# Softmax row sums inverted through 32x32 transposes on VectorE

## The chip, the cores and the metric

The kernel runs on one core of a Trainium2 chip. Its engines work side by side and each takes its own instructions in order: TensorE (PE in the profile; PEld is its weight load), VectorE (DVE), ScalarE (ACT), GpSimd (POOL), and SyncE (SP), which issues the DMAs. They meet through semaphores. The time is the device time of one execution in microseconds (us), and what is compared is the median of several executions.

## The reference

The input x is 8 images of 512 channels by 32x32 pixels, in fp32. With t the 1024 tokens of an image:

```
xn   = group_norm(x)                              # 32 groups
mask = sigmoid(relu(mean(xn) @ w1 + b1) @ w2 + b2) > 0.5      # per image and channel
hyp  = logmap0(mhsa(expmap0(xn * mask), hdn weights))
euc  = mhsa(xn * (1 - mask), eu weights)
out  = x + hyp + euc

mhsa(x): q, k, v = split(t @ w_qkv + b_qkv)       # 8 heads of 64
         attn    = softmax(q @ k.T / 8)           # 1024 x 1024 per head
         out     = (attn @ v) @ w_o + b_o
```

So there are 16 attentions (8 images, 2 branches), each with 8 heads. The change is about the softmax's denominator: one number per head and query, whose reciprocal multiplies the 64 outputs of that head and query.

## The kernel before, in words

The outer loops run over the image i (0 to 7) and the branch t (0 and 1). In a branch, heads go in 4 pairs and queries in 2 halves of 512, which makes 8 phases ph = 2 * pair + half; a phase has 8 key tiles of 128, and one unit g is one key tile for both heads of the pair. BATCHES is 32: a batch b is two units, so a phase lasts 4 batches. All engines follow the same hand-written timetable in b; nothing is planned at run time.

For each unit TensorE makes the scores (`scores`, L1449), ScalarE their exponentials (`exps`, L871, tile `probs`, 4 slots), TensorE multiplies them by v into `acc_ps` (`prob_v`, L1463), and GpSimd adds them up over the key tiles into `sums` (`probs_sum`, L690). In the same batches TensorE makes what the next pair needs: the q and k projections (`qk_tile`, L1364) and, in two slots per batch (`max_slot`, L1413), products whose row maxima VectorE takes (`mxp`, L1201). Both slots of a batch use the same two PSUM banks (0 and 1), so the second slot's matmuls wait for the first slot's reduction, and the first slot of the next batch waits for the second's. `combine` (L1211) and `turn` (L1224, eight 32x128 transposes) shape the maxima.

At the end of a phase, `denominator` (L1477) multiplies `sums` by a 128x64 matrix of ones into an auxiliary bank. Its output is 128 partitions by 512 queries, and the 64 partitions of one head all hold the same number. ScalarE copies it to `den` (`den_copy`, L882), VectorE inverts it in place (`recip`, L1285), GpSimd multiplies the drained attention output `o_raw` by it (`mult`, L697), ScalarE and VectorE split the product into a rounded part and a rest (`o_hi` L887, `o_lo` L1290), and the output projection (`o_tile`, L1364 with w_o) reads both. Output tiles 0 to 3 need the first query half, tiles 4 to 7 the second.

`recip` is called twice per phase, each time for 256 of the 512 columns, in batches 4 * ph + 6 and 4 * ph + 8 (the second call of phase 6 in batch 31), and behind the second max slot of the batch. Phase 7 is inverted behind the last batch, with all 512 columns in one call. VectorE's order in a batch:

```
max_slot, combine                        # first slot
o_lo, small steps, lows(b - 1)           # qk_lo of the projections
max_slot, combine                        # second slot
recip(ph, parts)                         # even batches, and 31
scale_x and other steps, turn
```

`Count.at(i, n)` turns "n-th event of image i" into a semaphore value; `c_rec` counts quarters of a phase's inversion (RECIP_PARTS = 4), and `mult` waits for all four. SyncE begins the program by incrementing each semaphore of the list COUNTS once (L520), before its first DMA (L566).

Of the kernel before, what the change touches and what calls it, by code (L numbers as in the profile page):

```python
# [13 lines left out]
P = 128  # L14
HALF = 512
# [3 lines left out]
PAIRS = HEADS // 2  # L19
# [43 lines left out]
BLOCK = 32  # L63
# [23 lines left out]
RECIP, RECIP_PARTS = [6, 8], 4  # L87
# [8 lines left out]
def followed(i):  # L96

    return i != B - 1
# [7 lines left out]
def wanted(i, t, p):  # L106

    return p < PAIRS or t != 1 or followed(i)
# [3 lines left out]
def max_slot_at(b, j):  # L112

    return divmod(2 * b + j - MAX_FROM, 16)
# [11 lines left out]
def phase_at(b, what):  # L126

    ph, r = divmod(b - what, 4)
    return ph if r == 0 and 0 <= ph < 2 * PAIRS - 1 else None
# [12 lines left out]
def projections(b):  # L142

    out = [("v", m) for m in range(2 * b, 2 * b + 4) if b % 2 == 0 and m < NT]
    for p in range(2, PAIRS + 2):
        out += [("qk", p, k) for k in range(4) if b == min(8 * p + QK_AT[k], BATCHES)]
    return out
# [81 lines left out]
def build(nc, x, w1, b1, w2, b2, hw_qkv, hb_qkv, hw_o, hb_o, ew_qkv, eb_qkv, ew_o, eb_o, out):  # L229
    ctx = ExitStack()  # L230
    with ctx:
        ctx.enter_context(nc.allow_non_contiguous_dma(reason="biases, once"))

        def sb(name, shape, dt=F32):
            return ctx.enter_context(nc.sbuf_tensor(name, shape, dt))
# [30 lines left out]
        den = sb("den", [P, 2, HALF])  # L266

        mxw = sb("mxw", [P, 2, NT // 2, BLOCK], F32R)
        mxp = sb("mxp", [P, 2, NT, 2])
        group_mean = sb("group_mean", [P, P])  # L270
        ones = sb("ones", [P, HD])
        stats = sb("stats", [P, KC, 2, 6])
# [23 lines left out]
        def frees(tiles, e, n=None):  # L296

            return sum(by == e for _, by, _ in tiles[:n])
# [8 lines left out]
        def sem(name):  # L307
            return ctx.enter_context(nc.semaphore(name))

        def counted(name, per, before=0):  # L310
            return Count(sem(name), per, before)
# [16 lines left out]
                 for q in range(XIN)]  # L328
# [16 lines left out]
        c_free = {e: counted(n, frees(AUX, e), frees(FIRST, e))  # L345
                  for e, n in (("A", "aux_read_by_scalar"), ("D", "aux_read_by_vector"),
                               ("Q", "qk_lo_made"))}
        c_hi = counted("qk_hi_made", 32, 8)
        c_mx = counted("max_made", 16, 2)

        c_turn = [counted(f"max_rows_made{h}", 8, 1 - h) for h in range(2)]
        c_neg = [counted(f"max_rows_rounded{h}", 8, 1 - h) for h in range(2)]
        c_score = counted("scores_made", NSC)
        c_exp = counted("probs_made", NSC)
        c_pv = counted("probs_multiplied", 2 * TILES)
        c_sum = [counted(f"probs_summed{h}", NSUM) for h in range(2)]
        c_raw = counted("o_drained", 16)
        c_rec = counted("recip_made", 16 * RECIP_PARTS)
        c_on = counted("o_normal", 16)
        c_ohi = counted("o_hi_made", 16)  # L360
        c_olo = counted("o_lo_made", 16)
        c_sq = counted("y_squared", 8)
# [3 lines left out]
        c_dstep = counted("vector_step", DVE_STEPS, DVE_FIRST)  # L366
        c_astep = counted("scalar_step", ACT_STEPS, ACT_FIRST)
        COUNTS = [*c_wqk, c_wv, c_wo, *c_xin, c_xfree, c_ss, c_yread, c_ysc, c_ysm, c_xlo, c_xm, c_xg, c_keep, c_xa, c_pe_in, c_d2a, c_a2d, c_yd2a, c_ya2d, c_aux,
                  *c_free.values(), c_hi, c_mx, *c_turn, *c_neg, c_score, c_exp, c_pv, *c_sum, c_raw, c_rec, c_on, c_ohi, c_olo, c_sq,
                  c_sqf, *c_x, *c_vst, c_dstep, c_astep]  # L370

        def bank(name):
# [7 lines left out]
        def aux_made(eng, i, name):  # L380

            eng.wait_ge(c_aux.sem, c_aux.at(i, at(i, name)[1] + 1))
            return bank(name)

        def aux_read(eng, i, name):

            tiles, n = at(i, name)
            e = tiles[n][1]
            eng.wait_ge(c_free[e].sem, c_free[e].at(i, frees(tiles, e, n + 1)))
# [37 lines left out]
        def token_half(h):  # L427
            return slice(h * HALF, (h + 1) * HALF)
# [24 lines left out]
        def y_square(k):  # L453

            return probs[:, SLOTS_P - 2 + k % 2, 0:HALF]
# [509 lines left out]
        def _(dve):  # L965
# [31 lines left out]
            def rows(ap):  # L997
                return ap.rearrange("p (r w) -> p r w", w=W)
# [278 lines left out]
            for i in range(B):  # L1277
                steps[0] = 0
                for t in range(2):

                    def recip(ph, parts):
                        n = 8 * t + ph
                        aux_read(dve, i, (t, "den", ph))
                        first, last = (parts[k] * HALF // RECIP_PARTS for k in (0, 1))
                        dve.reciprocal(den[:, ph % 2, first:last], den[:, ph % 2, first:last]).then_inc(c_rec.sem, parts[1] - parts[0])  # L1285

                    def o_lo(ph):
                        p, h = ph // 2, ph % 2
                        dve.wait_ge(c_ohi.sem, c_ohi.at(i, 8 * t + ph + 1))
                        dve.scalar_tensor_tensor(o_t[:, 1, p, token_half(h)], o_raw[:, ph % 2, :],  # L1290
                                                 bias_q[:, t, 2, p:p + 1], o_t[:, 0, p, token_half(h)].bitcast(F32),
                                                 ALU.add, ALU.subtract).then_inc(c_olo.sem, 1)

                    def lows(b):
                        for f in projections(b):
                            if f[0] == "qk" and wanted(i, t, f[1]):
                                qk_lo(i, t, f[1], f[2])

                    def y_done(k, t):
                        if t:  # L1300
                            ps = aux_made(dve, i, (1, "o", k))
                            dve.wait_ge(c_yread.sem, c_yread.at(i, k + 1))
                            dve.scalar_tensor_tensor(v_y[:, k, :], ps, bias_o[:, 1, k % KC:k % KC + 1], v_y[:, k, :],
                                                     ALU.add, ALU.add).then_inc(c_free["D"].sem, 1)
                        else:
                            dve.wait_ge(c_sq.sem, c_sq.at(i, k + 1))
                            dve.tensor_reduce(ss_y[:, k * ROWS:(k + 1) * ROWS], rows(y_square(k)), AX.X,
                                              ALU.add).then_inc(c_sqf.sem, 1)

                    for b in range(BATCHES):  # L1310
                        if t == 0 and b - 1 in GATE_BATCH and followed(i):
                            gate_read(i, t, GATE_BATCH[b - 1])
                        for j in range(2):
                            p, s = max_slot_at(b, j)
                            if wanted(i, t, p):
                                max_slot(i, t, p, s)
                                if s in HALF_DONE:
                                    combine(i, t, p, HALF_DONE.index(s))
                            if j == 0:
                                if t and b == Y_LAST:  # L1320
                                    y_done(7, 0)
                                if phase_at(b, LOW) is not None:
                                    o_lo(phase_at(b, LOW))
                                if t:
                                    y_scale_step(i, b)
                                    operand_step(i, t, b)
                                else:
                                    gate_step(i, b)
                                if b:
                                    lows(b - 1)  # L1330
                        for ph, parts in recips(b):
                            recip(ph, parts)
                        if t:
                            operand_tail(i, t, b)
                        else:
                            gate_tail(i, t, b)
                        if turn_at(b, TURN_AT) and wanted(i, t, turn_at(b, TURN_AT)[0]):
                            turn(i, t, *turn_at(b, TURN_AT))
                    o_lo(2 * PAIRS - 3)
                    lows(BATCHES - 1)  # L1340
                    o_lo(2 * PAIRS - 2)
                    lows(BATCHES)
                    if not closing(i, t):
                        y_done(0, t)
                    recip(2 * PAIRS - 1, (0, RECIP_PARTS))
                    if closing(i, t):
                        y_done(0, t)
                    y_done(1, t)
                    o_lo(2 * PAIRS - 1)
                    for k in range(2, 8 if t else 7):  # L1350
                        y_done(k, t)
                assert steps[0] == DVE_STEPS or not followed(i), ("DVE_STEPS", steps[0])
# [210 lines left out]
```

## Time and profile before

| | |
|---|---|
| median of 3 runs | 3894.97 us (3889.81 to 3895.17) |
| the profiled execution | 3897.88 us |
| its span, first to last instruction | 3896.1 us |
| TensorE busy | 3827.4 us (98%), 21164 matmuls |
| VectorE busy | 2651.4 us (68%), 3576 instructions |
| GpSimd busy | 2664.5 us (68%), 1300 instructions |
| ScalarE busy | 1917.2 us (49%), 3489 instructions |
| mean granted TensorE clock | 0.998 |

The span is the stretch that the profiler sees; 1.8 us of the execution lie outside it. Busy is time in which an engine has an instruction under way. A matmul's end is modelled, so for TensorE it is better to read the distance from one start to the next. "Idle before" is what an engine waited before an instruction, with the instruction that released it.

### The profile page before, as it was taken

The page shows a single profiled execution, that of the slowest core. Times are in us where ns is not written, and L with a number is a line of the kernel's source. Part 1 is how long each engine was busy: PE and PEld are TensorE (multiplying, and loading weights), DVE is VectorE, ACT ScalarE, POOL GpSimd, SP SyncE. Part 2 cuts the span into 40 slices and gives each one's busy share as a digit, 9 for nine tenths or more (in the row PEclk, how much of TensorE's full clock was granted, in tenths as well). Part 3 has the DMA queues.
Part 4 walks back from the last instruction along what each step waited for, and adds up shares of the span by engine and source line. Part 5 has one row for each costly group of instructions (what it writes and reads, how often), then busy time and mean ns, then how long its engine had stood idle before and what let it go on. Part 6 is the DMA issues. An engine that isn't in the chain of part 4 may idle for free.

```text
span 3896.1 us, 57425 instructions
## 1 busy us (share of the span) xinstructions
PE 3827.4 (98%) x21164; PEld 2396.8 (62%) x21164; DVE 2651.4 (68%) x3576; ACT 1917.2 (49%) x3489; POOL 2664.5 (68%) x1300
## 2 busy tenths in 40 slices
PE   5999999999999999999999999999999999999999
PEld 3656566565665656566565665656656565565655
DVE  6675856758667585676857668576785758847566
ACT  4455534545345553555535555354553545535444
POOL 4584876838668486774867658675586856858468
PEclk9999999999999999999999999999999999999999
DMA  8212132121321213212141121411213112121102
GB/s 286 103 44 98 33 98 82 44 98 33 101 79 50 98 33 112 73 49 91 35 146 45 50 82 33 146 47 52 76 49 130 49 49 76 57 95 44 66 12 66
DMA packets 137555, 293.14 MB, mean 75 GB/s; under 512 B 16704, under 2 KB 28992, under 8 KB 127296
## 3 DMA queue, kind: packets, MB, share of 16 engines
q1 hardware_dynamic: 137280, 289.47, 21.9%
q8 instruction: 173, 2.83, 0.3%
q14 instruction: 102, 0.84, 0.1%
HBM read 239.09 MB, written 50.33 MB: 74 GB/s over the span
## 4 chain that ended last, share of the span: by engine, by line
PE 93%; DVE 4%; POOL 1%; issue 1%; DMA 0%; ACT 0%; SPq 0%; POOLq 0%; DVEq 0%; ACTq 0%
PE aux_ps L1364 32%; PE score_ps L1449 22%; PE acc_ps L1463 22%; PE aux_ps L1413 8%; PE score_ps L1364 4%; PE aux_ps L1477 3%; DVE mxp L1201 2%; POOL sums L690 1%; DVE neg_max L1224 0%; DVE xin L1101 0%; DMA w_split<-w_o 0%; DVE sc L995 0%; PE aux_ps L1379 0%; PE aux_ps L1382 0%; DVE den L1285 0%
## 5 line engine op out<-in xcount | busy, mean ns | idle before, releaser
L690 POOL TENSOR_TENSOR sums<-sums,probs 128x1024 f32<-128x1024 f32 x765 | 1832.8, 2396 | 723.3 <-ACT probs L871 668.9
L1201 DVE TENSOR_REDUCE mxp<-aux_ps 128x2 f32<-128x1024 f32 x1014 | 1240.3, 1223 | 884.6 <-PE aux_ps L1413 874.5
L871 ACT ACTIVATE probs<-score_ps 128x512 f32<-128x512 f32 x2048 | 1059.7, 603 | 1001.8 <-PE score_ps L1449 730.0
L1463 PE MATMUL acc_ps<-probs,v_y 128*64 128x512 f32 x4096 | 955.3, 599 | 0.6 <-ACT probs L871 0.6
L1364 PE MATMUL aux_ps<-xs,w_qk 128*128 128x512 f32 x2976 | 753.4, 401 | 0.0
L1364 PEld LDWEIGHTS aux_ps<-xs,w_qk 128*128 128x128 f32 x2976 | 537.8, 188 | 195.2 <-issue 89.4
L1463 PEld LDWEIGHTS acc_ps<-probs,v_y 128*64 128x64 f32 x4096 | 270.3, 136 | 529.7 <-issue 388.7
L690 POOL TENSOR_TENSOR sums<-probs 128x1024 f32<-128x1024 f32 x128 | 306.4, 2393 | 339.6 <-ACT probs L871 339.2
L1413 PE MATMUL aux_ps<-k_hi,q_hi 64*128 64x512 f32 x2028 | 459.8, 446 | 20.2 <-DVE mxp L1201 17.9
L1285 DVE RECIPROCAL den<-den 128x256 f32<-128x256 f32 (+1 forms) x240 | 443.9, 1850 | 14.7 <-ACT den L882 13.3
L1449 PE MATMUL score_ps<-q_hi,k_hi 64*128 64x512 f32 x2048 | 409.7, 393 | 0.6 <-ACT q_max L811 0.6
L1449 PE MATMUL score_ps<-q_hi,k_lo 64*128 64x512 f32 x2048 | 407.8, 391 | 0.0
L1449 PE MATMUL score_ps<-q_lo,k_hi 64*128 64x512 f32 x2048 | 406.3, 390 | 0.0
L1449 PE MATMUL score_ps<-q_max,first_rows 64*128 64x512 f32 x2048 | 405.0, 388 | 0.0
L1413 PEld LDWEIGHTS aux_ps<-k_hi,q_hi 64*128 64x128 f32 x2028 | 194.7, 183 | 340.2 <-issue 276.3
L1364 PE MATMUL aux_ps<-o_t,w_o 128*128 128x512 f32 x1536 | 355.4, 390 | 0.0
L1364 PEld LDWEIGHTS aux_ps<-o_t,w_o 128*128 128x128 f32 x1536 | 287.1, 188 | 72.1 <-issue 13.0
L1224 DVE STREAM_TRANSPOSE neg_max<-mxw 32x128 f32<-32x128 f32 x1024 | 308.7, 301 | 12.4
L697 POOL TENSOR_TENSOR o_raw<-o_raw,den 128x512 f32<-128x512 f32 x128 | 171.0, 1337 | 110.5 <-DVE den L1285 110.5
L1449 PEld LDWEIGHTS score_ps<-q_lo,k_hi 64*128 64x128 f32 x2048 | 196.5, 184 | 41.5
L1449 PEld LDWEIGHTS score_ps<-q_max,first_rows 64*128 64x128 f32 x2048 | 195.8, 184 | 42.1
L1449 PEld LDWEIGHTS score_ps<-q_hi,k_lo 64*128 64x128 f32 x2048 | 195.3, 184 | 39.5
(139 smaller groups left out, 3193.3 us busy)
## 6 DMA issues: line engine op xcount, KB each, us to landing
w_qk<-w_split SPq DMA_DIRECT2D x124, 512.0 KB, 4.2
xin<-in_x_dram SPq DMA_DIRECT2D x232, 256.0 KB, 3.4
w_o<-w_split SPq DMA_DIRECT2D x32, 1024.0 KB, 8.1
w_v<-w_split SPq DMA_DIRECT2D x30, 1024.0 KB, 7.8
v_y<-in_x_dram SPq DMA_DIRECT2D x72, 256.0 KB, 3.2
y<-v_y SPq DMA_DIRECT2D x64, 256.0 KB, 2.0
xin<-y SPq DMA_DIRECT2D x64, 256.0 KB, 3.2
out_dram<-v_y SPq DMA_DIRECT2D x64, 256.0 KB, 6.5
```

The source lines that it names most:

```text
L690: pool.tensor_tensor(sums[h][:, :], a, probs[:, g % SLOTS_P, :], ALU.add).then_inc(c_sum[h].sem, 1)
L697: pool.tensor_tensor(o_raw[:, ph % 2, :], o_raw[:, ph % 2, :], den[:, ph % 2, :], ALU.mult).then_inc(c_on.sem, 1)
L871: act.activation(probs[:, n % SLOTS_P, token_half(u % 2)], score_ps[:, u % SCORE_BANKS, :], ACT.Exp, scale=SCALE).then_inc(c_exp.sem, 1)
L1201: dve.tensor_reduce(mxp[:, :, n, h], ps, AX.X, ALU.max).then_inc(c_free["D"].sem, 1)
L1224: made = dve.transpose(rows[at:at + BLOCK, :, BLOCK * a:BLOCK * (a + 1)], mxw[BLOCK * a:BLOCK * (a + 1), j, :, :].bitcast(F32))
L1285: dve.reciprocal(den[:, ph % 2, first:last], den[:, ph % 2, first:last]).then_inc(c_rec.sem, parts[1] - parts[0])
L1364: last = nc.tensor.matmul(ps, lhs(a, k), rhs(b, k), start=(j == 0), stop=(j == len(todo) - 1))
L1413: last = nc.tensor.matmul(ps[:, j, :], q_hi[head(j), p % 2, n * P:(n + 1) * P], k_hi[head(j), p % 2, token_half(h)], start=True, stop=True)
L1449: last = nc.tensor.matmul(score_ps[:, (2 * n + j) % SCORE_BANKS, :], lhs, qq[head(j), cols] if qq is q_max else qq[head(j), p % 2, cols], ...
L1463: last = nc.tensor.matmul(acc_ps[head(j), :], v_y[:, m, head(2 * p + j)], probs[:, n % SLOTS_P, token_half(j)], start=(m == 0), stop=(m == ...
L1477: last = nc.tensor.matmul(ps[head(j), :], ones[:, :], term[:, token_half(j)], start=(n == 0), stop=(n == len(terms) - 1))
```

## The change

Each `recip` becomes three instructions on VectorE. The first transposes every 32x32 block of the 128x256 stretch of `den` into `den_cols`. Since the 32 partitions of a block hold equal rows, the turned block has equal columns, and column 0 holds the block's 32 different numbers, one per partition. The second instruction inverts that column alone: 8 blocks, so 128x8 elements. The third reads each inverted element 32 times (a stride of 0) and transposes back into `den`. Two new semaphores order the three; VectorE waits for itself twice. The call for phase 7 becomes two calls of 256 columns, since `den_cols` holds 256.

```diff
+        den_cols = sb("den_cols", [P, HALF // BLOCK // 2, BLOCK])
+        den_inv = sb("den_inv", [P, HALF // BLOCK // 2])
...
+        c_dcol = counted("den_columns_made", 16 * RECIP_PARTS)
+        c_dinv = counted("den_columns_inverted", 16 * RECIP_PARTS)
...
-                  *c_free.values(), c_hi, c_mx, *c_turn, *c_neg, c_score, c_exp, c_pv, *c_sum, c_raw, c_rec, c_on, c_ohi, c_olo, c_sq,
+                  *c_free.values(), c_hi, c_mx, *c_turn, *c_neg, c_score, c_exp, c_pv, *c_sum, c_raw, c_rec, c_dcol, c_dinv, c_on, c_ohi, c_olo, c_sq,
...
                         first, last = (parts[k] * HALF // RECIP_PARTS for k in (0, 1))
-                        dve.reciprocal(den[:, ph % 2, first:last], den[:, ph % 2, first:last]).then_inc(c_rec.sem, parts[1] - parts[0])
+                        done, count = c_rec.at(i, RECIP_PARTS * n + parts[1]) - c_rec.at(i, 0), parts[1] - parts[0]
+                        cols = den[:, ph % 2, first:last]
+                        dve.transpose(den_cols[:, :, :].rearrange("p a c -> p (a c)"), cols).then_inc(c_dcol.sem, count)
+                        dve.wait_ge(c_dcol.sem, c_dcol.at(i, done))
+                        dve.reciprocal(den_inv[:, :], den_cols[:, :, 0]).then_inc(c_dinv.sem, count)
+                        dve.wait_ge(c_dinv.sem, c_dinv.at(i, done))
+                        dve.transpose(cols.rearrange("p (a c) -> p a c", c=BLOCK),
+                                      den_inv[:, :].unsqueeze(2).to_broadcast([P, HALF // BLOCK // 2, BLOCK])).then_inc(c_rec.sem, count)
...
-                    recip(2 * PAIRS - 1, (0, RECIP_PARTS))
+                    recip(2 * PAIRS - 1, (0, 2))
+                    recip(2 * PAIRS - 1, (2, 4))
```

## Rows read from the trace of the kernel before

**Rows 1.** The page's first part: busy us, share of the span, number of instructions.
```profile
PE 3827.4 (98%) x21164; PEld 2396.8 (62%) x21164; DVE 2651.4 (68%) x3576; ACT 1917.2 (49%) x3489; POOL 2664.5 (68%) x1300
```

**Rows 2.** The waits: who waited for whom, us in total, times, longest us.
```profile
POOL o_raw L697 <- DVE den L1285: 110.5, 31, 10.4
...
PE aux_ps L1413 <- DVE mxp L1201: 17.9, 34, 1.4
...
PE score_ps L1413 <- DVE mxp L1201: 4.3, 2, 3.2
```

**Rows 3.** VectorE's groups by line and shape: busy us, mean ns; idle before.
```profile
L1285 DVE RECIPROCAL den<-den 128x256 f32<-128x256 f32 x224 | 390.4, 1743 | 4.0 <-ACT den L882 2.6
...
L1285 DVE RECIPROCAL den<-den 128x512 f32<-128x512 f32 x16 | 53.6, 3348 | 10.7 <-ACT den L882 10.7
...
L1307 DVE TENSOR_REDUCE ss_y<-probs 128x16 f32<-128x512 f32 x64 | 43.8, 684 | 84.3 <-ACT probs L944 84.2
...
L1211 DVE TENSOR_REDUCE mxw<-mxp 128x8 fp32r<-128x16 f32 x128 | 22.1, 173 | 4.4
```

**Rows 4.** The tile neg_max: its transposes, duration in ns as minimum/median/maximum.
```profile
L1224 DVE STREAM_TRANSPOSE neg_max<-mxw x1024: 241/303/309, 79.4 to 3834.2; 32x128 f32<-32x128 f32 x171
```

**Rows 5.** Timeline: start us, us, what, [idle before]; two instructions with a wait between.
```profile
1580.72 0.16 DVE L1031 TENSOR_TENSOR small<-mv,gm 128x4 f32<-128x4 f32 x1
...
1580.92 0.16 DVE L1032 TENSOR_TENSOR small<-small 128x4 f32<-128x4 f32 x1
```

**Rows 6.** Timeline of image 2, branch 1, at batches 20 and 21.
```profile
1429.27 1.74 DVE L1285 RECIPROCAL den<-den 128x256 f32<-128x256 f32 x1
...
1429.78 0.50 PE L1413 MATMUL aux_ps<-k_hi,q_hi 64*128 64x512 f32 x2
...
1430.93 1.16 DVE L1201 TENSOR_REDUCE mxp<-aux_ps 128x2 f32<-128x1024 f32 x1
...
1431.74 0.40 PE L1449 MATMUL score_ps<-q_max,first_rows 64*128 64x512 f32 x2
...
1432.23 0.50 PE L1413 MATMUL aux_ps<-k_hi,q_hi 64*128 64x512 f32 x2
```

**Rows 7.** Timeline: the same place in image 0, the first of the eight.
```profile
474.53 1.15 DVE L1201 TENSOR_REDUCE mxp<-aux_ps 128x2 f32<-128x1024 f32 x1
...
475.14 0.40 PE L1449 MATMUL score_ps<-q_max,first_rows 64*128 64x512 f32 x2
...
475.83 0.50 PE L1413 MATMUL aux_ps<-k_hi,q_hi 64*128 64x512 f32 x2 [0.30 <-DVE mxp L1201]
```

**Rows 8.** Timeline: such a place in image 7, the last of the eight.
```profile
3817.49 0.43 PE L1449 MATMUL score_ps<-q_max,first_rows 64*128 64x512 f32 x2
...
3818.34 0.50 PE L1413 MATMUL aux_ps<-k_hi,q_hi 64*128 64x512 f32 x2 [0.42 <-DVE mxp L1201]
```

**Rows 9.** Timeline of a branch's tail, with the inversion of phase 7.
```profile
1506.52 19.34 PE L1364 MATMUL aux_ps<-o_t,w_o 128*128 128x512 f32 x84
...
1507.33 3.35 DVE L1285 RECIPROCAL den<-den 128x512 f32<-128x512 f32 x1 [0.96 <-ACT den L882]
...
1512.85 0.77 DVE L1290 SCALAR_TENSOR_TENSOR o_t<-o_raw,bias_q,o_t 128x512 fp32r<-128x512 f32 x1 [1.59 <-ACT o_t L887]
```

**Rows 10.** Timeline of the program's start: SyncE's first DMAs.
```profile
4.51 3.71 SPq L566 DMA_DIRECT2D v_y<-in_x_dram  x8
```

**Rows 11.** The tile sc: two-input VectorE instructions, ns as minimum/median/maximum.
```profile
L1101 DVE TENSOR_TENSOR xin<-xin,sc x56: 683/693/1952, 422.1 to 3352.0; 128x512 f32<-128x512 f32 x56
...
L995 DVE TENSOR_TENSOR sc<-sc x8: 291/1396/2502, 37.2 to 3284.0; 128x128 f32<-128x128 f32 x8
```

**Rows 12.** Timeline of image 0, branch 1, batch 11: such an instruction held up.
```profile
415.18 4.86 POOL L690 TENSOR_TENSOR sums<-sums,probs 128x1024 f32<-128x1024 f32 x2 [0.50 <-ACT probs L871]
415.19 2.50 DVE L995 TENSOR_TENSOR sc<-sc 128x128 f32<-128x128 f32 x1
...
419.75 0.51 PE L1413 MATMUL aux_ps<-k_hi,q_hi 64*128 64x512 f32 x2 [1.11 <-DVE mxp L1201]
```

## Prediction, written before the changed kernel was run

> **What bounds the kernel now.** I read the busy shares first: TensorE is busy 3827.4 us of 3896.1, VectorE only 2651.4 [rows 1]. So time is saved on VectorE only where TensorE stands waiting for it. The second view is the list of waits. TensorE waits for VectorE's row maxima 34 times for 17.9 us and twice for 4.3 us in score banks [rows 2]; no wait of TensorE names the inversion itself. GpSimd does wait for the inversion, 110.5 us in 31 waits [rows 2], but GpSimd is busy at 68% [rows 1] and its multiplication feeds work that, in the tails, has slack (below). So 17.9 + 4.3 = 22.2 us is the ceiling of what a faster VectorE can give, 0.6% of the time, start-up included. The third view is the timeline around each such wait, to see what VectorE had been doing before.
>
> **The change, part by part.**
>
> *Removed.* 224 inversions of 256 columns at 1743 ns and 16 of 512 at 3348 ns, 443.9 us of VectorE [rows 3].
>
> *Added, the two transposes.* The trace has none of 128x256. Its 32x128 transposes take 303 ns, between 241 and 309 [rows 4]. For the slope I take the two reductions with 512 and 16 elements per partition: (684 - 173) / 496 = 1.03 ns per element [rows 3]. That gives 303 + 128 * 1.03 = 435 ns. The ends are far apart: at the bottom 173 ns, the shortest of these rows, if columns were free; at the top the cost by blocks, 8 times as many 32x32 blocks as a 32x128 transpose has (32 against 4), 8 * 303 = 2424 ns, if blocks were turned one after another. I take 435, since in these rows durations follow the elements per partition and not the number of partitions.
>
> *Added, the small inversion.* (3348 - 1743) / 256 = 6.27 ns per element and 138 ns fixed [rows 3], so 8 elements are 138 + 50 = 188 ns. Its ends are 138 and, if a stride of 128 bytes doubled the element cost, 238 ns.
>
> *Added, the two waits on itself.* Two small instructions with such a wait start 0.20 us apart and last 0.16 [rows 5], so 0.04 us each, between 0 and 0.1.
>
> The chain is then 435 + 40 + 188 + 40 + 435 = 1138 ns, against 1743: 0.61 us saved per half phase. VectorE's busy time falls by 443.9 - 256 * 1.058 = 173 us, to about 2478 us. With the ends of all terms the chain lies between 0.48 and 5.2 us.
>
> The Trainium skill (VectorE: DVE Perf Modes, section on the TRN2 errata) says that each VectorE instruction with its source in SBUF pays a fixed latency, about 150 cycles as measured there, and its rules for kernel authors say to keep the number of instructions small, not the number of semaphores. The rule speaks against turning one instruction into three. By its measured formula, (N + 151) / 0.96, the transposes would be 424 ns each and the small inversion at least 166, a chain of 1.01 us by that estimate, still below 1.74. The 173 ns of the 16-element reduction agree with it; that waits are free does not agree with the 0.20 us distance.
>
> *What of it is on TensorE's path.* The tight place is a pair of max slots: TensorE's second slot waits for VectorE to reduce the first. Take image 2: the inversion starts at 1429.27, TensorE's slot is issued at 1429.78 and is ready about 0.5 us later, but the reduction starts only at 1430.93, straight behind the inversion; TensorE's next slot starts at 1432.23, 0.49 us after the last score matmul at 1431.74 [rows 6]. Undisturbed, that distance is 0.22 us, so 0.27 us are lost. In image 0 it is 475.14 to 475.83, so 0.47 lost [rows 7], in image 7 3817.49 to 3818.34, so 0.63 [rows 8]. Going through all places where a max slot starts over 0.1 us late, some 40, I find an inversion straight ahead of the reduction in 8 of them, one per image, in branch 1 around batch 20; the eight losses are together 3.2 us. With a chain 0.61 us shorter, the reduction of image 2 starts when TensorE's slot is ready, near 1430.3, and ends near 1431.5, ahead of the 1431.96 at which TensorE wants its bank. In image 0 it ends at 475.68 - 0.61 = 475.07, before 475.36. In image 7 it is 3817.57 against 3817.71, which just does. So all eight go: -3.2 us. Next late there would be TensorE's own stream. The other late places stand behind row sums of squares, turns, and two-input instructions held up by GpSimd; those do not move with the inversion.
>
> In all other places the shorter chain is hidden: VectorE then waits for the next slot's matmuls instead.
>
> *The tail, in two calls.* The single inversion takes 3.35 us from 1507.33, and the rest part for the second half is ready at 1512.85 + 0.77 = 1513.62 [rows 9]. TensorE runs 84 matmuls in 19.34 us without a gap, 0.23 each; output tile 4 is behind 36 of them, at 1506.52 + 8.3 = 1514.8. So 1.2 us of slack exist already, and two chains (2.3 us) only make it 2.2. Worth nothing, and it would take a tail 1.2 us longer before it cost something. The wait of GpSimd for the inversion lies mostly here and goes with the same cover.
>
> *Two more semaphores.* SyncE's first DMA is issued at 4.51 us, behind some 63 increments [rows 10]: at most 0.07 us each, so +0.1 us.
>
> *Sum.* -3.2 + 0.1 = -3.1 us. On the profiled execution: 3897.88 - 3.1 = 3894.8. The median of the runs shown lies 2.9 us below that execution, so the forecast for the median is 3894.97 - 3.1 = 3891.9 us. A measurement here can tell about 0.2%, 7.8 us, from no change; the three runs alone spread over 5.4 us.
>
> **Rivals.**
>
> *A. The new instructions get stuck behind GpSimd (slower).* Two-input VectorE instructions on SBUF last from 683 to 1952 ns and from 291 to 2502 ns [rows 11]; one of them began 0.01 us after a GpSimd addition and took 2.50 us instead of 0.29, and TensorE lost 1.2 us behind it [rows 12]. If a 128x256 transpose from SBUF to SBUF were held up in the same way, it would decide from the point where a chain gets longer than 1.74 us. With GpSimd busy at 68%, about a quarter of such instructions would be hit in full, so 0.45 * 224 = 100 chains, 1.2 us each: +120 us, 4015. Against it: 1024 transposes of 32x128 never took over 309 ns [rows 4] beside the same GpSimd. The Trainium skill (SBUF — State Buffer, section "Who interferes with whom") says that VectorE and GpSimd share one port pair, taken by an instruction with two SBUF inputs or in a two-port mode for its whole length; copies may enter such a mode, transposes are not listed. The maximum of 309 ns agrees. Chance 0.04.
>
> *B. Blocks are turned one after another (slower).* The chain is 5.1 us, 3.4 more than now; with some 0.8 us of slack at each place, 224 * 2.6 = +580 us, about 4475. Nothing but the missing row speaks for it. Chance 0.02.
>
> *C. VectorE's load matters everywhere (faster).* A VectorE 173 us lighter would clear every wait of TensorE for maxima: -22.2, so 3872.8. For it: the waits are VectorE's. Against it: four of five late places have other work ahead of them. Chance 0.04, and 0.06 more for part of it, beyond -7.8.
>
> *D. The collision flips.* The stall of 1.2 us [rows 12] occurs in four of eight images (the first is shown), decided by 0.01 us. A small shift could give it to all or none: +-4.7 us around the forecast, 3887.2 to 3896.6. Both stay almost inside 0.2%. It widens the forecast's own range; a chance of 0.04 to leave it at the fast end.
>
> *E. Nothing moves*, since the changed order costs elsewhere what the eight places give: 3895.0. It belongs to the same band as the forecast; 0.25 of the 0.80 left.
>
> That the change doesn't do what it says I exclude but for its speed: the ones matrix has 64 columns per head, so all 32 rows of a block are equal.
>
> **How the numbers follow.** The forecast, with E, has 0.80, and lies within 0.2%. Faster by more than that: C with 0.10, D with 0.04, so 0.14. Slower: A and B with 0.06. The range takes the forecast with D's shift and some run-to-run spread: 3884 to 3898 us; A, B and the far part of C stay outside it.
>
> **What would show it.** Right: 512 transposes of about 0.43 us and 256 inversions of about 0.19 us in VectorE's groups; VectorE busy near 2478 us; TensorE's waits for maxima down from 34 by about 8; the eight places with 0.22 us between score and slot; GpSimd's wait for the inversion shorter, and the end no earlier for that. Wrong: transposes with a maximum far over their median (A), transposes over 0.8 us (B), waits gone also where no inversion stood ahead (C).

## The result, and the profile after

The changed kernel takes 3905.92 us, median of 8 runs (3900.75 to 3910.17); the kernel before, beside it on the same chip, 3895.01 us, median of 8 (3889.81 to 3896.76). The ratio is 1.0029, 95% interval 1.0021 to 1.0037: slower, by 10.9 us (8.2 to 14.4). The forecast was 3891.9 us with a range up to 3898, and slower had a chance of 0.06. It was wrong.

One trap first. The profiled execution after took 3900.75 us, the lowest of its 8 runs; the one before took 3897.88 us, above all 8 runs beside which it stands. Between the two traces lie only 2.9 of the 10.9 us, so the traces were compared place by place and not by their totals. Two things that vary from one execution to the next account for most of the rest: the trace before has the stall of [rows 12] in four images and the trace after in one (1.18 us each, 3.5 us in all), and its start-up, up to 105 us, takes 2.6 us longer.

The first part of the page, after (busy us, share of the span, instructions), against [rows 1]:

```profile
PE 3824.1 (98%) x21164; PEld 2395.2 (61%) x21164; DVE 2512.9 (64%) x4104; ACT 1918.3 (49%) x3489; POOL 2662.0 (68%) x1300
```

VectorE is 138.5 us lighter, and the kernel is slower. VectorE's groups of the change, and two that it does not touch (busy us, mean ns, idle before):

```profile
L1303 DVE SCALAR_TENSOR_TENSOR o_t<-o_raw,bias_q,o_t 128x512 fp32r<-128x512 f32 x128 | 143.6, 1122 | 95.3 <-ACT o_t L893 95.3
...
L1297 DVE STREAM_TRANSPOSE den<-den_inv 128x256 f32<-128x256 f32 x256 | 114.0, 445 | 28.0 <-DVE den_inv L1295 1.4
...
L1293 DVE STREAM_TRANSPOSE den_cols<-den 128x256 f32<-128x256 f32 x256 | 111.0, 433 | 15.2 <-ACT den L888 13.4 <-DVE sc_y L993 0.5
...
L1107 DVE TENSOR_TENSOR xin<-xin,sc 128x512 f32<-128x512 f32 x56 | 78.3, 1408 | 0.7
...
L1295 DVE RECIPROCAL den_inv<-den_cols 128x8 f32<-128x8 f32 x256 | 52.3, 204 | 27.5 <-DVE den_cols L1293 1.4
```

The three new groups take 277 us for 444 removed. The two untouched ones grew: `o_lo` (L1303) from 999 to 1122 ns and `scale_x` (L1107) from 1180 to 1408 ns, together 28.5 us. Both are two-input instructions. (`scale_x` multiplies a 512-column chunk of the next operand by its factors, in place; there are eight chunks, 0 to 7, for each of the first seven images.) The tile `sc` shows how `scale_x` spreads (ns as minimum/median/maximum), and it is to be read beside [rows 11]: the maximum went from 1952 to 2805. The median went from 693 to 1121, but it is a poor witness: it is 1119 in e10_waits_before below, which loses nothing.

```profile
L1107 DVE TENSOR_TENSOR xin<-xin,sc x56: 683/1121/2805, 418.2 to 3354.0; 128x512 f32<-128x512 f32 x56
```

The waits after (us in total, times, longest), to be read against [rows 2]:

```profile
POOL o_raw L703 <- DVE den L1297: 100.1, 16, 10.2
...
PE aux_ps L1427 <- DVE mxp L1207: 21.3, 35, 1.9
...
PE aux_ps L1378 <- DVE o_t L1303: 3.4, 7, 0.5
...
PE score_ps L1427 <- DVE mxp L1207: 1.4, 2, 1.1
```

TensorE's waits for maxima went up, 34 to 35 times and 17.9 to 21.3 us, and there is a wait that the list before did not have: 7 times for `o_t`. They are the two halves of the loss. GpSimd waits for the inversion in 16 places instead of 31; in the other 15 it is now released earlier.

**First half: batches 21 and 22 of branch 1.** Timeline after, image 2 (start us, us, what, [idle before]); it answers to [rows 6]:

```profile
1427.34 0.43 DVE L1293 STREAM_TRANSPOSE den_cols<-den 128x256 f32<-128x256 f32 x1
...
1427.65 0.50 PE L1427 MATMUL aux_ps<-k_hi,q_hi 64*128 64x512 f32 x2
...
1427.87 0.20 DVE L1295 RECIPROCAL den_inv<-den_cols 128x8 f32<-128x8 f32 x1
...
1428.18 0.45 DVE L1297 STREAM_TRANSPOSE den<-den_inv 128x256 f32<-128x256 f32 x1
...
1428.55 1.19 DVE L1207 TENSOR_REDUCE mxp<-aux_ps 128x2 f32<-128x1024 f32 x1
...
1429.61 0.40 PE L1463 MATMUL score_ps<-q_max,first_rows 64*128 64x512 f32 x2
...
1429.88 0.51 PE L1427 MATMUL aux_ps<-k_hi,q_hi 64*128 64x512 f32 x2
...
1431.00 5.15 POOL L696 TENSOR_TENSOR sums<-sums,probs 128x1024 f32<-128x1024 f32 x2
...
1437.48 5.19 POOL L696 TENSOR_TENSOR sums<-sums,probs 128x1024 f32<-128x1024 f32 x2
1437.64 2.80 DVE L1107 TENSOR_TENSOR xin<-xin,sc 128x512 f32<-128x512 f32 x1
1437.75 0.51 PE L1427 MATMUL aux_ps<-k_hi,q_hi 64*128 64x512 f32 x2 [0.63 <-DVE mxp L1207]
...
1440.36 1.21 DVE L1207 TENSOR_REDUCE mxp<-aux_ps 128x2 f32<-128x1024 f32 x1
...
1441.71 0.50 PE L1427 MATMUL aux_ps<-k_hi,q_hi 64*128 64x512 f32 x2 [0.49 <-DVE mxp L1207]
```

The same place before, from GpSimd's addition in batch 21 on:

```profile
1432.93 5.15 POOL L690 TENSOR_TENSOR sums<-sums,probs 128x1024 f32<-128x1024 f32 x2
...
1439.56 0.69 DVE L1101 TENSOR_TENSOR xin<-xin,sc 128x512 f32<-128x512 f32 x1
1439.68 0.50 PE L1413 MATMUL aux_ps<-k_hi,q_hi 64*128 64x512 f32 x2 [0.23 <-DVE mxp L1201]
1439.81 5.25 POOL L690 TENSOR_TENSOR sums<-sums,probs 128x1024 f32<-128x1024 f32 x2 [0.48 <-ACT probs L871]
...
1443.05 0.50 PE L1413 MATMUL aux_ps<-k_hi,q_hi 64*128 64x512 f32 x2
```

The batch-21 stall is gone but for 0.04 us, as predicted: 0.27 us between score and slot (1429.61 to 1429.88), where an undisturbed pair has 0.23. In image 7 it is not gone: 0.40 us are left of 0.85. Measured from batch 21's first slot, TensorE's second slot comes 2.23 us later instead of 2.45. But two slots on, in the second slot of batch 22, it comes 10.10 us later (1427.65 to 1437.75) instead of 9.90 (1429.78 [rows 6] to 1439.68): what was recovered is lost again, and more. And the slot after that is 3.96 us away (1437.75 to 1441.71) instead of 3.37. The reason for this second loss stands in the rows: before, `scale_x` started 0.25 us ahead of GpSimd's addition and took 0.69 us; after, the addition starts 0.16 us ahead of `scale_x`, which then takes 2.80 us, and the reduction that TensorE wants sits behind it. GpSimd's addition in batch 21 shows which of the two moved: counted from it, `scale_x` of batch 22 starts 6.63 us later before and 6.64 after (1432.93 to 1439.56, 1431.00 to 1437.64), but GpSimd's own addition of batch 22 starts 6.88 us later before and 6.48 after. The Trainium skill (SBUF — State Buffer, "Who interferes with whom") says that two-input VectorE instructions and GpSimd's reads share a port pair that is held for a whole instruction, and that the order of issue decides who is blocked; these rows agree, with 0.69 against 2.80 us.

**Second half: the tail of branch 1.** Timeline after, image 2:

```profile
1495.14 1.70 POOL L703 TENSOR_TENSOR o_raw<-o_raw,den 128x512 f32<-128x512 f32 x1
1496.03 5.75 PE L1378 MATMUL aux_ps<-xs,w_qk 128*128 128x512 f32 x24
...
1500.29 1.29 POOL L715 TENSOR_TENSOR v_y<-v_y,xin 128x512 f32<-128x512 f32 x1
1500.43 1.69 DVE L1303 SCALAR_TENSOR_TENSOR o_t<-o_raw,bias_q,o_t 128x512 fp32r<-128x512 f32 x1 [4.73 <-ACT o_t L893]
...
1502.27 3.00 PE L1378 MATMUL aux_ps<-o_t,w_o 128*128 128x512 f32 x12 [0.49 <-DVE o_t L1303]
```

And before:

```profile
1496.67 1.64 POOL L697 TENSOR_TENSOR o_raw<-o_raw,den 128x512 f32<-128x512 f32 x1 [0.59 <-DVE den L1285]
1497.11 5.75 PE L1364 MATMUL aux_ps<-xs,w_qk 128*128 128x512 f32 x24
...
1501.51 0.75 DVE L1290 SCALAR_TENSOR_TENSOR o_t<-o_raw,bias_q,o_t 128x512 fp32r<-128x512 f32 x1 [4.35 <-ACT o_t L887]
1501.76 1.65 POOL L709 TENSOR_TENSOR v_y<-v_y,xin 128x512 f32<-128x512 f32 x1
1502.70 1.52 PE L1364 MATMUL aux_ps<-o_t,w_o 128*128 128x512 f32 x6
```

`mult(6)`, the multiplication of phase 6, waited 0.59 us for the inversion before. Now it does not wait, and GpSimd runs 0.45 us earlier against TensorE (1495.14 - 1496.03 is -0.89 us, it was 1496.67 - 1497.11 = -0.44). The additions to `v_y` that GpSimd makes behind it, in the tail of branch 1, come earlier too, while `o_lo(6)` is tied to TensorE's projections: ScalarE's part of `o_t`, which releases it, starts 3.66 us behind them in both traces. Before, `o_lo(6)` led the addition by 0.25 us and took 0.75; now the addition leads by 0.14 and `o_lo(6)` takes 1.69. The first output tile starts 6.24 us after the projections (1496.03 to 1502.27), not 5.59: 0.65 us lost per image.

The sum from the traces: in the tail, from the last slot ahead of it to the first behind it, TensorE takes 33.70 us before and 34.43 to 34.47 after in each of seven images, together 5.3 us; 0.65 us of each stand ahead of the first output tile. In image 7, whose branch 1 ends the program and has another order there, the nearest `o_lo` starts 2.2 us ahead of the addition in both traces, and nothing changes places. From batch 21's first slot to batch 24's it takes 19.36 to 19.62 us before and 20.36 to 20.39 after in six images, 0.92 us more in the mean. Image 1 is the exception: there `scale_x` kept the lead, by 0.08 us, took 0.69 us, and the stretch got 0.38 us shorter. Image 7 has no `scale_x` in batch 22 and keeps the 0.42 us that it recovered. So this half is 5.1 - 0.4 = 4.7 us in the trace shown, and 6.0 where all seven images lose, as in the trace of e4_not6 below. Together that is 10.0 to 11.3 us, against 10.9 (8.2 to 14.4) measured. Why image 1 differs stays open: it keeps its 0.69 us in the traces of e6_wait and e12_after_again too, there with a lead of 0.01 us and without the stall of [rows 12].

### The profile page after: what moved, and what is told of

It reads as the page before. It is cut to its first block, busy times and chain, and to the rows that moved or that the text cites. A ratio compares the mean times of both kernels' runs of the same rounds, so it can differ in the third digit from the quotient of the medians.

```text
span 3899.0 us, 58483 instructions
## 1 busy us (share of the span) xinstructions
PE 3824.1 (98%) x21164; PEld 2395.2 (61%) x21164; DVE 2512.9 (64%) x4104; ACT 1918.3 (49%) x3489; POOL 2662.0 (68%) x1300
## 4 chain that ended last, share of the span: by engine, by line
PE 92%; DVE 4%; issue 1%; POOL 1%; DMA 1%; ACT 0%; SPq 0%; DVEq 0%; POOLq 0%; ACTq 0%
PE aux_ps L1378 31%; PE score_ps L1463 23%; PE acc_ps L1477 22%; PE aux_ps L1427 8%; PE score_ps L1378 4%; PE aux_ps L1491 3%; DVE mxp L1207 2%; POOL sums L696 1%; DVE xin L1107 0%; DVE neg_max L1230 0%; DVE o_t L1303 0%; DMA w_split<-w_o 0%; PE aux_ps L1393 0%; PE aux_ps L1396 0%; DMA v_y<-in_x_dram 0%
## 5 line engine op out<-in xcount | busy, mean ns | idle before, releaser
L1427 PE MATMUL aux_ps<-k_hi,q_hi 64*128 64x512 f32 x2028 | 459.5, 446 | 23.1 <-DVE mxp L1207 21.3
L1463 PEld LDWEIGHTS score_ps<-q_hi,k_hi 64*128 64x128 f32 x2048 | 194.5, 185 | 34.3 <-issue 8.4
```

What stands on the lines that cost most here:

```text
L1427: last = nc.tensor.matmul(ps[:, j, :], q_hi[head(j), p % 2, n * P:(n + 1) * P], k_hi[head(j), p % 2, token_half(h)], start=True, stop=True)
L1463: last = nc.tensor.matmul(score_ps[:, (2 * n + j) % SCORE_BANKS, :], lhs, qq[head(j), cols] if qq is q_max else qq[head(j), p % 2, cols], ...
```

## The experiments

All were timed in five rounds beside the kernel before on the same chip; its medians were 3889.76 us (first four), 3891.03 (next four) and 3890.42 (last four).

### Is it the new instructions, or the time they save?

**e1_pad** keeps every instruction and semaphore of the change and makes the small inversion as long as the saving:

```diff
-        den_inv = sb("den_inv", [P, HALF // BLOCK // 2])
+        den_inv = sb("den_inv", [P, HALF // BLOCK // 2, 10])
-   dve.reciprocal(den_inv[:, :], den_cols[:, :, 0])
+   dve.reciprocal(den_inv[:, :, :], den_cols[:, :, 0:10])
```

> The changed kernel with its small inversion widened from 8 to 80 elements per partition, into a scratch tile: by 6.27 ns per element the chain grows by 0.45 us, back to the 1.66 us that the old inversion held VectorE. Phase theory (the loss comes from VectorE and GpSimd meeting at other moments, because the inversion ends 0.45 us earlier): back to the time of before, 3895 +-3 us, ratio 0.9985 to 1.0008 to the kernel before, and TensorE no longer waits for o_t at the first output tile. Cost theory (three instructions, two waits and two semaphores cost by themselves): still 3906 or slower, ratio 1.003 or more.

Measured: 3892.45 us, ratio 1.0006 (0.9997 to 1.0015). The group shows the longer inversion (653 ns, so the chain is some 1.73 us with its gaps):

```profile
L1295 DVE RECIPROCAL den_inv<-den_cols 128x80 f32<-128x80 f32 x256 | 167.2, 653 | 27.5 <-DVE den_cols L1293 1.4
```

TensorE does not wait for `o_t`, and `scale_x` is back at a mean of 1192 ns. Three instructions, two waits and one more call per branch cost nothing that can be told from noise. What costs is that the result is ready earlier.

**e2_short** is the converse: the kernel before, with an inversion of about the changed chain's length and no transposes. It leaves out 72 of every 256 columns (136 of 512), which stay uninverted, so its output is wrong and only its time is of use.

```diff
+   some = first + (184 if last - first == 256 else 376)
-   dve.reciprocal(den[:, ph % 2, first:last], den[:, ph % 2, first:last])
+   dve.reciprocal(den[:, ph % 2, first:some], den[:, ph % 2, first:some])
```

> The kernel before, but its inversion covers only 184 of 256 columns (376 of 512), so it lasts 1.29 us like the chain of three without being one; 72 (136) columns of each stretch stay uninverted. Phase theory: as slow as the changed kernel, 3901 to 3908 us, ratio 1.002 to 1.0035, with seven waits of TensorE for o_t of some 0.65 us. Cost theory: nothing is lost and the eight places of the prediction are gained, 3892 us, ratio 0.999.

Measured: 3900.35 us, ratio 1.0029 (1.0018 to 1.0041), the loss of the change itself. `scale_x` has a mean of 1438 ns, and the waits (us in total, times, longest) show the one for `o_t`:

```profile
PE aux_ps L1414 <- DVE mxp L1201: 25.9, 39, 1.9
...
PE aux_ps L1365 <- DVE o_t L1291: 2.9, 7, 0.4
```

So the loss belongs to the earlier end, whatever instruction makes it.

### Which inversions?

**e3_phase6** turns phase 6 only, in both branches; the others are inverted as before, and phase 7 in one call. **e4_not6** turns all but phase 6. (Both also count the two new semaphores by the turned calls alone; that is not shown.)

```diff
+   if not (ph == 6):                    # e4_not6: if not (ph != 6):
+       dve.reciprocal(cols, cols).then_inc(c_rec.sem, count)
+       return
```

> Only the two inversions of phase 6 (batches 30 and 31) are turned, all others are as before. If the early multiplication of phase 6 lets GpSimd's y additions get ahead of VectorE's o_lo in the tail of branch 1: seven waits of 0.65 us for o_t, +4.5 us, ratio 1.0010 to 1.0013. If the tail has nothing to do with it: 3895, ratio 1.000.

Measured: 3896.31 us, 1.0017 (1.0008 to 1.0026). Its list of waits has the tail's mark in full; those for maxima are as before, 34:

```profile
PE aux_ps L1432 <- DVE mxp L1207: 18.3, 34, 1.4
...
PE aux_ps L1383 <- DVE o_t L1309: 3.4, 7, 0.5
```

> All inversions but those of phase 6 are turned. Phase theory: the loss of the tail (4.5 us) is gone, that around batches 20 to 22 stays, with a size between 0 and +6 us: 3897 to 3902 us, ratio 1.0005 to 1.0018. If the tail is not involved: 3906 as the changed kernel.

Measured: 3895.66 us, 1.0016 (1.0007 to 1.0025). No wait for `o_t`; the maxima have 20.4 us in 34 waits and `scale_x` a mean of 1438 ns. The two halves add up: 0.0017 + 0.0016 = 0.0033, inside the interval of the whole.

**e5_keep20** also leaves the inversion of batch 20 as it was, the one whose shortening was to bring the gain:

```diff
+   if not (ph != 6 and (ph, parts) != (3, (2, 4))):
+       dve.reciprocal(cols, cols).then_inc(c_rec.sem, count)
+       return
```

> All inversions turned but those of phase 6 and the one of batch 20 (phase 3, second half). Race theory: in batch 22 of branch 1 VectorE's scale_x wins the port from GpSimd's addition by 0.25 us before (starts 1 us apart from nothing else); the recovered stall of batch 21 moves scores and exponentials, and so the addition, 0.36 us forward, and VectorE loses. With the old inversion in batch 20 only 0.13 us are recovered, VectorE keeps the port by some 0.1 us: the waits of 0.8 and 0.6 us behind batch 21 are gone, ratio 0.9990 to 1.0004. Rival, the many shorter inversions together shift the phase: still 1.0016.

Measured: 3891.55 us, 1.0003 (0.9994 to 1.0011). One call per branch fewer than in e4_not6, and its loss is gone. Timeline of e5_keep20, image 2:

```profile
1424.85 1.74 DVE L1296 RECIPROCAL den<-den 128x256 f32<-128x256 f32 x1
1424.90 2.39 POOL L696 TENSOR_TENSOR sums<-probs 128x1024 f32<-128x1024 f32 x1
1425.17 0.50 PE L1433 MATMUL aux_ps<-k_hi,q_hi 64*128 64x512 f32 x2
...
1427.81 0.51 PE L1433 MATMUL aux_ps<-k_hi,q_hi 64*128 64x512 f32 x2 [0.27 <-DVE mxp L1207]
...
1428.50 5.14 POOL L696 TENSOR_TENSOR sums<-sums,probs 128x1024 f32<-128x1024 f32 x2
1429.57 1.83 DVE L1107 TENSOR_TENSOR xin<-xin,sc 128x512 f32<-128x512 f32 x1
...
1435.24 0.50 PE L1433 MATMUL aux_ps<-k_hi,q_hi 64*128 64x512 f32 x2 [0.20 <-DVE mxp L1207]
```

The long inversion and TensorE's stall behind it are back, and `scale_x` of batch 22 takes 0.69 us again. The other 208 calls are turned, and neither gain nor cost.

### Can a wait on GpSimd mend it?

**e6_wait** has GpSimd wait for `o_lo(6)` before its tail additions.

```diff
+   if k == 0 and not closing(i, t):
+       pool.wait_ge(c_olo.sem, c_olo.at(i, 8 * t + 7))
    y_sum(k)
```

> The changed kernel, and GpSimd starts the y additions of a branch-1 tail only when VectorE's o_lo of phase 6 is done. Race theory: the seven waits of TensorE for o_t are gone, some 4.5 us less than the changed kernel, ratio to before 1.0014 to 1.0018 (as the kernel with phase 6 left alone). Rival, the wait lies with the early multiplication itself or GpSimd now is late for the output tiles: 1.0029 or more.

Measured: 3895.65 us, 1.0012 (1.0003 to 1.0021). The waits for `o_t` are gone and the maxima's are not (20.3 us, 34): what remains is the batch-22 half, the same as e4_not6 within the intervals. The ratio, 1.0012, lies a little under the 1.0014 to 1.0018 that was expected.

**e7_both** also moves `scale_x(7)` behind the inversion of batch 22; **e8_moved_before** is the kernel before with that move alone.

```diff
-SCALE_AT, SCALE_TAIL = {12: (0,), 14: (1, 2), 18: (4,), 19: (5,), 22: (7,)}, {15: (3,), 21: (6,)}
+SCALE_AT, SCALE_TAIL = {12: (0,), 14: (1, 2), 18: (4,), 19: (5,)}, {15: (3,), 21: (6,), 22: (7,)}
```

> The same, and scale_x of chunk 7 is moved behind the second max slot of batch 22. Race theory: no max slot waits behind that instruction any more; gone are 0.8 + 0.6 + 0.1 us per image of the changed kernel and the 0.39 us that the kernel before lost there too: 1.1 to 1.3 us per image below before, ratio 0.9972 to 0.9985. Rival, another late place takes over: 1.000 or more.

Measured: 3897.57 us, 1.0018 (1.0009 to 1.0027). A miss.

> The kernel before with only scale_x of chunk 7 moved: what the move gives without a shorter inversion. It frees 0.39 + 0.11 us per image in seven images: ratio 0.9989 to 0.9995. If the tail of batch 22, now 1.7 us of inversion and 0.7 to 2.4 us of scale_x, is too long for TensorE's 2.7 us of projection: 1.000 to 1.002.

Measured: 3900.62 us, 1.0024 (1.0014 to 1.0033). The move cures nothing: `scale_x` now meets GpSimd there (2.15 us in e8_moved_before, 2.19 in e7_both, in image 2) and batch 22's tail gets too long. By the distances of TensorE's slots that costs 1.33 us per image with the long inversion and 0.88 to 1.07 with the short one. Here, and in image 7, a faster inversion is seen to pay, about 0.4 us per image, the size of its saving; the medians lie 3.05 us apart, though the intervals overlap and e7_both has the wait of e6_wait besides.

**e9_waits** takes e6_wait and orders the other race too: GpSimd begins batch 22's additions only behind `scale_x(7)`. **e10_waits_before** gives the same two waits to the kernel before.

```diff
+   if t and b == 22 and followed(i):
+       pool.wait_ge(c_xg.sem, c_xg.at(i, 8))
    for g in (2 * b, 2 * b + 1):
```

> The changed kernel with both races decided by waits of GpSimd: in the tail of branch 1 its y additions start behind VectorE's o_lo of phase 6, and in batch 22 its next addition starts behind VectorE's scale_x of chunk 7. Race theory: seven waits for o_t gone, the 0.6 and 0.1 us behind batch 22 gone and the 0.8 there back at 0.39; what remains is the recovered 0.3 us per image: 1.5 to 3 us below before, ratio 0.9990 to 0.9998. Rival, the waits make GpSimd late and the loss moves there: 1.0005 or more.

Measured: 3891.63 us, 1.0002 (0.9993 to 1.0011). The loss is gone, the hoped-for gain is not there. Timeline of e9_waits, image 2:

```profile
1427.24 2.40 POOL L696 TENSOR_TENSOR sums<-probs 128x1024 f32<-128x1024 f32 x1
1427.49 0.50 PE L1431 MATMUL aux_ps<-k_hi,q_hi 64*128 64x512 f32 x2
...
1429.73 0.49 PE L1431 MATMUL aux_ps<-k_hi,q_hi 64*128 64x512 f32 x2
...
1430.84 5.16 POOL L696 TENSOR_TENSOR sums<-sums,probs 128x1024 f32<-128x1024 f32 x2
1431.50 2.27 DVE L1111 TENSOR_TENSOR xin<-xin,sc 128x512 f32<-128x512 f32 x1
...
1437.48 0.69 DVE L1111 TENSOR_TENSOR xin<-xin,sc 128x512 f32<-128x512 f32 x1
1437.60 0.50 PE L1431 MATMUL aux_ps<-k_hi,q_hi 64*128 64x512 f32 x2 [0.63 <-DVE mxp L1211]
```

`scale_x(7)` is first and takes 0.69 us. The rows also show why nothing is gained; put them beside those of e5_keep20. From batch 21's first slot to its second TensorE takes 2.24 us here and 2.64 there: the stall is recovered, 0.40 us. But GpSimd's two additions are 3.60 us apart in both (1427.24 to 1430.84, 1424.90 to 1428.50), and batch 21's `scale_x`, held up by the later of them, ends 2.93 us after that addition's start here and 2.90 there. VectorE's stream hangs on GpSimd's at this place, and GpSimd's has not moved. So TensorE's slot in batch 22 comes 10.11 us after the first one here (1427.49 to 1437.60) and 10.07 there: the 0.40 us are waited out two slots later. The kernel with the same waits and all inversions long, e10_waits_before, says the same: from GpSimd's first addition to TensorE's slot in batch 22 it takes 10.35 us (1425.23 to 1435.58), and 10.36 here (1427.24 to 1437.60). Only image 7, with no `scale_x` behind the stall, keeps what it recovers, 0.42 us.

> The kernel before with the same two waits, as a control: both races were won by VectorE there anyway, so nothing changes, ratio 0.9996 to 1.0004, and the difference to the kernel above is what the shorter inversion is worth, 1.5 to 3 us.

Measured: 3891.12 us, 1.0002 (0.9993 to 1.0011). The waits cost nothing measurable on the kernel before either. With both races ordered, the two inversions are worth the same within the intervals, and the 1.5 to 3 us that both expectations gave the short one are missing.

**e11_three** adds one more wait, for the collision of [rows 12]:

```diff
+   if t and b == 11 and followed(i):
+       pool.wait_ge(c_dstep.sem, c_dstep.at(i, 31))
```

> The same as the first with a third wait: in batch 11 GpSimd's addition starts behind the last step of VectorE's x_blend, which in some images waited 2.2 us for the port and cost TensorE 1.2 us. If that race is lost in the timed executions too, up to seven times 1.2 us are saved: ratio 0.9972 to 0.9990. If it is lost mainly in profiled ones: as the first, 0.9990 to 0.9998.

Measured: 3891.67 us, 1.0004 (0.9995 to 1.0013). Nothing to gain. The stall of [rows 12] does not appear in the traces of the kernels from e4_not6 on, with or without this wait. The traces that have it in four or five images are of executions well above their medians (e2_short 3908.51 us against 3900.35, e1_pad 3898.33 against 3892.45, e3_phase6 3900.81 against 3896.31). So in these later measurements it seems to make single executions longer and hardly to touch a median. In the first one it may have: both medians there, 3895.01 and 3905.92, lie 4 to 5 us above those taken later, the size of four stalls, and no trace tells whether it is that stall or the chip. Why it comes in some executions stays open.

**e12_after_again** is the changed kernel once more, beside the last three.

> The changed kernel once more, on this chip, beside its mended versions: ratio 1.0021 to 1.0037 as measured first, and again seven waits for o_t and some six of 0.8 us in batch 22 in its profile.

Measured: 3900.62 us, 1.0027 (1.0016 to 1.0037), with the same marks (`o_t` 3.4 us in 7 waits, maxima 20.3 us in 34). The loss repeats on another occasion, at 10.2 us. No version was faster than the kernel before.

## Why the prediction was wrong

Right, or nearly:
- *The transposes*: 435 ns predicted, 433 and 445 measured, 512 of them. By the Trainium skill's formula (VectorE: DVE Perf Modes, section on the TRN2 errata), which the page gives for an fp32 addition of two tensors, an estimate would be 424; the trace is 2 to 5% above.
- *The small inversion*: 188 ns predicted, 204 measured.
- *Rivals A and B*: no transpose lasted over 449 ns beside a GpSimd at 68%, and blocks do not add up.
- *The batch-21 stalls* went in seven images, to 0.23 to 0.27 us between score and slot; in image 7 0.40 us are left of 0.85. e5_keep20, which has the long inversion back there (and in phase 6), has them again.
- *SyncE*: the first DMA is issued at 4.62 us instead of 4.51, the 0.1 predicted. *The end of the tail in two calls* costs nothing, as said: e5_keep20 has it, at 1.0003.

Off in size:
- *The two waits on itself*: 0.04 us each predicted. In the chain ahead of batch 21's first slot the gaps are 0.10 and 0.11 us (1427.34 + 0.43 to 1427.87; 1427.87 + 0.20 to 1428.18), and the overlap of about 0.08 us between neighbours without a wait is lost at each. From its start to the next instruction the chain takes 1.21 us, the inversion took 1.66 [rows 6]: 0.45 us saved, not 0.61. That was enough for seven of the eight stalls and not for image 7, whose margin was worked out with 0.61. (The upper end of the chain is 5.3 us by its own terms, not 5.2; nothing hangs on it.)
- *VectorE's busy time*: 2478 us predicted, 2512.9 measured. 28.5 us of the 35 are the longer `o_lo` and `scale_x`, which the sum held constant; the rest is the three new groups, 277 us and not 271.

Failed:
- *"In all other places the shorter chain is hidden: VectorE then waits for the next slot's matmuls instead."* This looked only at VectorE as the late one. An instruction that ends earlier also releases others earlier. Here the recovered time moves TensorE's scores, by them ScalarE's exponentials, and by them GpSimd's addition in batch 22, while `scale_x` is held by what GpSimd did in batch 21. Two arrivals 0.25 us apart changed places. e4_not6 against e5_keep20 shows it (1.0016 against 1.0003, whose intervals touch; in the traces `scale_x` of batch 22 takes 2.8 us in all seven images of the one and 0.69 in all seven of the other), and e9_waits shows that ordering the two is enough to take the loss away.
- *"The other late places stand behind row sums of squares, turns, and two-input instructions held up by GpSimd; those do not move with the inversion."* They do. The batch-22 place is such a one, two slots behind the batch-21 stall, and it takes back what that stall gave: the term of -3.2 us was real where it was read, and where the next wait ends only the 0.42 us of image 7 are left of it, too little to be told in the times (e9_waits and e10_waits_before, both 1.0002).
- *"The wait of GpSimd for the inversion lies mostly here and goes with the same cover."* The slack was worked out for phase 7 and output tile 4 only. For phase 6 the wait was 0.59 us, and what matters there is not whether `mult(6)` is late but what GpSimd does next when it is early: its additions to `v_y` against `o_lo(6)`. e3_phase6 has this half alone (1.0017), and e6_wait removes it.

Rival D had the right kind of mechanism, a collision that flips by a small shift, but only for the one place where a stall stood in the trace of before, and at both signs. What it missed is that the collisions to fear are those that before *wins* narrowly, and they leave no wait in any list.

## What to carry to other kernels

Before an edit makes something earlier, follow what it releases, not only what it delays: list the two-input VectorE instructions that start just ahead of a GpSimd operation on the same SBUF, and ask which of the pair moves. If the lead is smaller than the shift, count the loss of the race (here 2.80 us instead of 0.69, and 1.69 instead of 0.75). A recovered stall is a gain only if the engines behind the next wait move too; look two or three waits further down for one that hangs on an engine which has not moved.

## What the runs showed of the hardware

- A 128x256 fp32 transpose from SBUF to SBUF takes 433 ns, 445 with its source broadcast along the free dimension. The tile `den` over all 256 (minimum/median/maximum):

```profile
L1297 DVE STREAM_TRANSPOSE den<-den_inv x256: 445/445/449, 145.8 to 3876.3; 128x256 f32<-128x256 f32 x128
L1293 DVE STREAM_TRANSPOSE den_cols<-den x256: 401/434/447, 145.0 to 3875.5; 128x256 f32<-128x256 f32 x128
```

- It is untouched by GpSimd's work beside it (maximum 449 ns of 512), where two-input instructions of 0.7 us took up to 2.8.
- A wait of VectorE for its own last instruction costs about 0.10 us and the 0.08 us of overlap, here 0.18 us per wait. Without them the three instructions would by these numbers hold VectorE for 1.08 - 3 * 0.08 = 0.84 us instead of 1.66, an estimate; of that saving of 0.82 us the two waits took 0.36, and 0.45 are left.
- Being first by 0.14 to 0.25 us decides a race for 0.9 to 2.1 us, and it is decided the same way in seven of seven images of the tail and in six or seven of seven in batch 22: so it shows as a loss and not as scatter. The narrowest leads seen, 0.01 us for `scale_x` in image 1 of e6_wait and e12_after_again, were enough to keep its 0.69 us.
